# One call order in the self-attention loop: the finishing steps of a head group move behind the row-maximum steps

## The chip, the cores and the metric

The kernel runs on one core of a Trainium2 chip, in one launch. The metric is the device time of that core in microseconds (us). The kernel before takes 2647.46 us as the median of three runs (2645.61 to 2647.74).

## The reference, cut to what matters

The program computes two layers on 8 batch elements of 512 tokens with 512 features: a cross-attention layer (L0) on 77 context tokens, and then a block of self-attention, a second cross-attention and an MLP, all in float32. The change touches the self-attention alone. Its part of the reference is:

```python
NH = 16; hd = H // NH; scale = hd ** (-0.5)           # 16 heads of 32
x_norm = modulate(_ln(x), shift_a, scale_a)
q, k, v = jnp.split(x_norm @ W_qkv + b_qkv, 3, axis=-1)
attn_w = jax.nn.softmax(jnp.einsum('bhqd,bhkd->bhqk', q, k) * scale, axis=-1)   # 512 x 512 per head
attn_out = jnp.einsum('bhqk,bhkd->bhqd', attn_w, v)
attn_out = attn_out.transpose(0, 2, 1, 3).reshape(B, N, H) @ W_proj + b_proj
x = x + gate_a[:, None] * attn_out
```

## The kernel before, in words

Every engine is given its own instruction stream. One description of the order of the work (the `run` method of each stage) is walked once for each engine; each walk calls that engine's version of the same steps, and the engines meet only at semaphores. `braid` takes one step of each generator that it is given, in the order of its arguments, then the next step of each. The order of the arguments is therefore the order in which an engine finds the instructions of one step in its queue, and each engine works its queue strictly in that order.

The self-attention (class `SelfAttention`) works through 32 head groups n = 4b + g: batch element b, and four of the 16 heads in each g. A group has 16 steps (4 tiles of 128 keys or queries x 4 heads), numbered 0 to 15 here. In the braid of group n there run side by side:

- `attend(n)`: TensorE makes the scores of one key tile and head (L1871) into one of two PSUM banks, ScalarE takes their exponentials (L1949). Before steps 2, 6, 10 and 14 TensorE also makes the value sums of the key tile that is complete (L1893, with L1905 for the row sums of exponentials before steps 2 and 10), and GpSimd adds pairs of exponential tiles (L1751), one before step 10 and one at the start of the next group, right after the last exponential of this one. At the end of groups with g = 0 (from n = 4 on) GpSimd also adds the bias to the residual rows, in four instructions (L1734).
- `maxima(n + 2)`: TensorE makes the scores of the group after next the other way round (L1850) into a ring of three banks, VectorE reduces each to its negated row maxima (L1785). TensorE may write a bank again once VectorE has reduced it.
- `max_rows(n + 1)` at step 2: the maxima of the next group are turned by TensorE (L1859, which takes a bank of the same ring), copied by ScalarE (L1934), subtracted by VectorE (L1791) and sent by DMA into row 96 and 97 of the query stack.
- `finish(n - 1)`: the normalisation of the group before. ScalarE copies the value sums out of PSUM at step 2 (L1962). VectorE turns the row sums at step 10 (L1799), takes reciprocals at step 11 (L1802), spreads them at step 12 (L1805) and multiplies at step 13 (L1811). ScalarE rounds the product to the first part of a two-part number at step 14 (L1971), which stands in its queue between the exponentials of steps 14 and 15. VectorE makes the second part at step 15 (L1816).
- `project(b - 1)` in groups with g = 1, 2 and 3 from b = 1 on: the output projection of the batch element before (L389 on TensorE, gating on VectorE at L1830, adding on GpSimd at L1760). It is spread over the steps, 3 or 6 matmuls a step.

The rings that bind the engines are made in one line each:

```python
self.scores, self.max_banks, self.products = k.ring(0, 1), k.ring(2, 3, 4), k.ring(5)
self.heads, self.sums = k.ring(6), k.ring(7)
```

In ScalarE's `finish` the wait for VectorE's product stands ahead of the rounding copy:

```python
for _ in range(12):
    yield
act.wait_ge(*self.normalised(n))
...
e.copy(k.o[n % 6][:, 0, :], k.o_wide[n % 2][:]).then_inc(self.heads_hi.sem, 1)
```

Of the kernel before, what the change touches and what calls it, by code (L numbers as in the profile page):

```python
# [29 lines left out]
LAST = len(SEQ)  # L30
# [75 lines left out]
def braid(*generators):  # L106

    left = [g for g in generators if g is not None]
    while left:
        for g in list(left):  # L110
            if next(g, StopIteration) is StopIteration:
                left.remove(g)
        if left:
            yield
# [7 lines left out]
def after(steps, generator):  # L122
    for _ in range(steps):
        yield
    yield from generator


def some(steps, generator):
    for _ in range(steps):
        next(generator, None)  # L130
        yield
# [284 lines left out]
class Prepare:  # L416
# [90 lines left out]
    def run(self, s, following):  # L507
        def splits(l, first, n):
            for i in range(first, first + n):
                s.split(self.piece_at[l] + i)  # L510
                yield

        def modulations(*sources):
            for i in sources:
                yield from s.modulation(i)

        s.begin()
        s.statistics()
        yield from braid(s.context(0), after(2, splits(1, 0, G)), after(2, modulations(0)))
        yield from braid(s.keys(0), splits(1, G, G), after(1, modulations(1)))  # L520
        yield from braid(s.values(0), modulations(2, 3), some(10, following))
        yield from braid(s.context(1), some(4, following))
        yield from braid(some(9, following), splits(0, 0, 2 * G))
        yield from s.keys(1)
        yield from s.values(1)
# [1059 lines left out]
class SelfAttention:  # L1585
# [45 lines left out]
    def run(self, s, following):  # L1631

        for n in range(self.FETCH):
            s.fetch(n)
        s.load_values(0)
        yield
        yield from s.maxima(0)
        yield from braid(s.maxima(1), after(4, s.max_rows(0)))
        for n, (b, g) in enumerate(SEQ):
            if n < G:  # L1640
                s.split(self.wp_at + n)
            if n + 1 < LAST:
                s.load_values(n + 1)
            if n + self.FETCH < LAST:
                s.fetch(n + self.FETCH)
            side = []
            if g == 1 and b > 0:
                s.add_base(b - 1)
                projecting = s.project(b - 1)
            if g > 0 and b > 0:  # L1650
                tiles = (0, 1, 2, 1)[g]
                part = after(4 if g == 1 else 0, some(tiles * 4, projecting))
                side += [part] * tiles
            if n >= LAST - G - 1:
                side.append(some((1, 5, 3, 6, 8)[n - LAST], following))
            yield from braid(s.attend(n), s.finish(n - 1) if n else None, s.maxima(n + self.MAX) if n + self.MAX < LAST else None,
                             after(2, s.max_rows(n + self.ROWS)) if n + self.ROWS < LAST else None, *side)
            if g == 0 and b > 0:
                s.load_base(b - 1)
        s.values(LAST - 1, NT - 1)  # L1660
        s.sum_pair(LAST - 1, 1)
        s.load_base(B - 1)
        yield from s.finish(LAST - 1)
        yield from some(12, following)
        s.add_base(B - 1)
        yield from s.project(B - 1)
# [685 lines left out]
```

## Time and profile before

| | |
|---|---|
| median of three runs | 2647.46 us |
| the profiled execution's own time | 2647.46 us |
| its span in the trace | 2645.7 us |
| TensorE busy (matmul) | 2426.7 us, 92% |
| VectorE busy | 1388.3 us, 52% |
| ScalarE busy | 1024.6 us, 39% |
| GpSimd busy | 581.1 us, 22% |
| self-attention, first score to first score of the last group | 868.7 to 1457.1 us |

The span is the stretch that the trace covers; 1.8 us of the execution's own time lie outside it. TensorE is the engine that the chain of work that ended last runs through for 75% of the span. A busy share is an average over stages with different limits, so what an edit is worth has to be read in the self-attention stage itself. "PE" is TensorE's matmuls, "PEld" its weight loads, "DVE" VectorE, "ACT" ScalarE, "POOL" GpSimd.

### The profile page before, as it was taken

The page shows a single profiled execution, that of the slowest core. Times are in us where ns is not written, and L with a number is a line of the kernel's source. Part 1 is how long each engine was busy: PE and PEld are TensorE (multiplying, and loading weights), DVE is VectorE, ACT ScalarE, POOL GpSimd, SP SyncE. Part 2 cuts the span into 40 slices and gives each one's busy share as a digit, 9 for nine tenths or more (in the row PEclk, how much of TensorE's full clock was granted, in tenths as well). Part 3 has the DMA queues.
Part 4 walks back from the last instruction along what each step waited for, and adds up shares of the span by engine and source line. Part 5 has one row for each costly group of instructions (what it writes and reads, how often), then busy time and mean ns, then how long its engine had stood idle before and what let it go on. Part 6 is the DMA issues. An engine that isn't in the chain of part 4 may idle for free.

```text
span 2645.7 us, 32309 instructions
## 1 busy us (share of the span) xinstructions
PE 2426.7 (92%) x12048; PEld 1696.1 (64%) x12048; DVE 1388.3 (52%) x2463; ACT 1024.6 (39%) x1831; POOL 581.1 (22%) x325
## 2 busy tenths in 40 slices
PE   6678999979998899999998789999889999999998
PEld 5556666658886444444444456666578888888887
DVE  4456655464445787777777456666543222222221
ACT  2534444333332455555554233343433332332231
POOL 2001111110000356666665312111111011001100
PEclk9889999999999899999999899999999999999999
DMA  6477766645546455655553476586441101100110
GB/s 229 133 175 204 227 196 192 178 164 182 183 176 186 128 132 130 152 141 136 123 147 89 120 184 199 163 220 182 154 130 60 41 16 56 56 26 31 56 41 16
DMA packets 261227, 354.19 MB, mean 134 GB/s; under 512 B 60931, under 2 KB 109147, under 8 KB 261070
## 3 DMA queue, kind: packets, MB, share of 16 engines
q1 hardware_dynamic: 259902, 348.27, 46.2%
q0 software_dynamic: 1168, 3.85, 0.4%
q8 instruction: 96, 1.57, 0.3%
q14 instruction: 61, 0.50, 0.1%
HBM read 233.78 MB, written 116.69 MB: 132 GB/s over the span
## 4 chain that ended last, share of the span: by engine, by line
PE 75%; DVE 8%; DMA 5%; ACT 5%; issue 3%; SPq 2%; POOL 1%; DVEq 0%; ACTq 0%; POOLq 0%
PE banks L389 39%; PE banks L2150 13%; PE banks L1871 6%; PE banks L1893 4%; PE banks L1850 4%; PE banks L1905 2%; DMA norm_x<-x 1%; PE banks L1304 1%; PE banks L350 1%; PE banks L1290 1%; PE banks L1311 1%; DMA q_parts_self<-out_parts 1%; ACT wide L373 1%; DVE x_rows L1233 1%; DVE negated_max L1190 1%
## 5 line engine op out<-in xcount | busy, mean ns | idle before, releaser
L1949 ACT ACTIVATE self_exponentials<-banks 128x512 f32<-128x512 f32 x512 | 286.2, 594 | 286.3 <-PE banks L1905 137.4
L1785 DVE TENSOR_REDUCE negated_max<-banks 128x1 f32<-128x512 f32 x512 | 328.8, 676 | 104.7 <-PE banks L1850 103.2
L1751 POOL TENSOR_TENSOR self_exponentials<-self_exponentials,self_exponentials 128x2048 f32<-128x2048 f32 x64 | 294.0, 4593 | 213.7 <-ACT self_exponentials L1949 213.7
L2150 PE MATMUL banks<-mlp_w_down_hi,out_parts 128*128 128x512 f32 x1024 | 333.8, 389 | 0.1
L2106 DVE TENSOR_TENSOR out_parts<-wide,out_parts 128x512 fp32r<-128x512 f32 x128 | 93.0, 726 | 378.6 <-ACT out_parts L2179 378.6
L2169 ACT ACTIVATE wide<-banks,bias_columns 128x512 f32<-128x512 f32 x128 | 88.3, 690 | 428.0 <-PE banks L389 428.0
L1871 PE MATMUL banks<-self_query_stack,self_key_stack 98*128 98x512 f32 x512 | 234.4, 459 | 12.7 <-ACT self_exponentials L1949 6.2
L1850 PE MATMUL banks<-self_key_stack,self_query_stack 96*128 96x512 f32 x512 | 207.5, 411 | 17.8 <-DVE negated_max L1785 8.3
L1871 PEld LDWEIGHTS banks<-self_query_stack,self_key_stack 98*128 98x128 f32 x512 | 97.7, 191 | 194.8 <-ACT self_exponentials L1949 152.7
L2150 PEld LDWEIGHTS banks<-mlp_w_down_hi,out_parts 128*128 128x128 f32 x1024 | 192.2, 188 | 40.4 <-DVE x_rows L1233 0.5
L333 POOL TENSOR_SCALAR norm_rstd<-norm_mean_var 128x4 f32<-128x4 f32 x32 | 8.7, 273 | 911.1 <-DVE norm_mean_var L312 910.6
L2150 PE MATMUL banks<-mlp_w_down_lo,out_parts 128*128 128x512 f32 x512 | 199.2, 389 | 0.0
L1190 DVE TENSOR_REDUCE negated_max<-banks 128x4 f32<-128x308 f32 x256 | 120.6, 471 | 91.7 <-PE banks L389 86.8
L1893 PE MATMUL banks<-self_exponentials,self_values 128*32 128x512 f32 x1024 | 138.2, 612 | 0.5 <-ACT self_exponentials L1949 0.5
L1176 DVE SCALAR_TENSOR_TENSOR out_parts<-banks,bias_columns,out_parts 128x512 fp32r<-128x512 f32 x64 | 47.8, 747 | 145.7 <-ACT out_parts L1348 145.7
L1850 PEld LDWEIGHTS banks<-self_key_stack,self_query_stack 96*128 96x128 f32 x512 | 99.3, 194 | 36.9 <-DVE negated_max L1785 15.2
L1372 ACT ACTIVATE cross_exponentials<-banks 77x512 f32<-77x512 f32 x128 | 75.3, 591 | 122.8 <-PE banks L1290 122.6
L308 DVE BATCH_NORM_STATS2 norm_stats<-norm_x 128x6 f32<-128x512 f32 x128 | 84.6, 671 | 67.6 <-DMA norm_x<-x 61.9
L373 ACT ACTIVATE wide<-banks,modulation_columns 128x512 f32<-128x512 f32 x96 | 74.4, 775 | 108.5 <-PE banks L350 101.6
L1372 ACT ACTIVATE L_exponentials<-banks 77x512 f32<-77x512 f32 x128 | 75.3, 591 | 99.7 <-PE banks L1290 99.5
L1563 ACT ACTIVATE out_parts<-banks,bias_columns 128x512 fp32r<-128x512 f32 x64 | 44.1, 689 | 176.4 <-PE banks L389 153.7
L1149 POOL TENSOR_TENSOR x_rows<-x_rows,cross_projection_bias 128x512 f32<-128x512 f32 x32 | 44.2, 1413 | 306.0 <-DMA x_rows<-x 306.0
(201 smaller groups left out, 5405.1 us busy)
## 6 DMA issues: line engine op xcount, KB each, us to landing
L_query_stack<-q_parts_L SPq DMA_DIRECT2D x96, 256.0 KB, 4.7
x<-x_rows SPq DMA_DIRECT2D x24, 1024.0 KB, 5.0
norm_x<-x SPq DMA_DIRECT2D x24, 1024.0 KB, 7.6
self_query_stack<-q_parts_self SPq DMA_DIRECT2D x96, 256.0 KB, 4.0
self_key_stack<-k_parts_self SPq DMA_DIRECT2D x96, 256.0 KB, 6.3
x_rows<-x SPq DMA_DIRECT2D x24, 1024.0 KB, 6.1
cross_query_stack<-q_parts_cross SPq DMA_DIRECT2D x96, 256.0 KB, 4.7
q_parts_L<-out_parts SPq DMA_DIRECT2D x32, 512.0 KB, 3.9
```

Source lines behind the costliest of these rows:

```text
L373: e.activation(k.wides[w][:], bank, ACT.Identity, **kw).then_inc(self.wide.sem, 1)
L389: mm = e.matmul(out_ap, l, r, start=i == 0, stop=i == len(terms) - 1)
L1190: e.tensor_reduce(k.nm[n % 2][:, t:GH * NT:NT], k.bank[:, bk, 0:GH * S].rearrange("p (h k) -> p h k", k=S), AX_X, ALU.max, negate=True).th ...
L1372: e.activation(self.p[:, i % self.HEADS_KEPT, :], k.bank[0:S, self.scores.of["score", i], :], ACT.Exp, scale=SCALE).then_inc(self.exp.sem, 1)
L1751: e.tensor_tensor(self.p[kt - 1][:], self.p[kt - 1][:], self.p[kt][:], ALU.add).then_inc(self.paired.sem, 1)
L1785: e.tensor_reduce(k.nm[n % 2][:, h * NT + t:h * NT + t + 1], k.bank[:, self.max_banks.of["max", i], :], AX_X, ALU.max, negate=True).then_i ...
L1850: e.matmul(k.bank[:, bk, :], self.q[n % 4][0:ST, h, t * P:(t + 1) * P], self.keys[n % 4][0:ST, h, :], start=True, stop=True).then_inc(self ...
L1871: e.matmul(k.bank[:, bk, :], self.keys[n % 4][0:ST_MAX, h, kt * P:(kt + 1) * P], self.q[n % 4][0:ST_MAX, h, :], start=True, stop=True).the ...
L1893: mm = e.matmul(k.bank[h * HD:(h + 1) * HD, bk, :], self.v[n % 3][:, kt, h * HD:(h + 1) * HD], self.p[kt][:, h, :], start=kt == 0, stop=kt ...
L1949: e.activation(self.p[kt][:, h, :], k.bank[:, self.scores.of["score", i], :], ACT.Exp, scale=SCALE).then_inc(self.exp.sem, 1)
L2106: e.tensor_tensor(h[:, 1, :], k.wides[k.wide_turns.of["up", i]][:], raw(h[:, 0, :]), ALU.subtract).then_inc(self.lo.sem, 1)
L2150: mm = e.matmul(bank, l, w, start=j == 0 and q == 0, stop=j == JC - 1 and q == 2)
```

## The change

`finish(n - 1)` is passed to `braid` behind `maxima` and `max_rows` and no longer ahead of them. Nothing else is edited, and no instruction is added or dropped.

```diff
-            yield from braid(s.attend(n), s.finish(n - 1) if n else None, s.maxima(n + self.MAX) if n + self.MAX < LAST else None,
-                             after(2, s.max_rows(n + self.ROWS)) if n + self.ROWS < LAST else None, *side)
+            yield from braid(s.attend(n), s.maxima(n + self.MAX) if n + self.MAX < LAST else None,
+                             after(2, s.max_rows(n + self.ROWS)) if n + self.ROWS < LAST else None,
+                             s.finish(n - 1) if n else None, *side)
```

The queues of TensorE, GpSimd and SyncE (which issues the DMAs) hold the same instructions in the same order as before, since `finish` has nothing on them. VectorE's and ScalarE's queues change. (The edit is one line longer, so lines behind it have numbers higher by one in the changed kernel.)

On VectorE, in one group (here a group without projection), steps 3 to 15 before. `negated_max` are the reductions of `maxima`; `sums_turned`, `reciprocals_turned`, `heads_float` and `heads_parts` are the finishing instructions.

```order
L1785 TENSOR_REDUCE negated_max_83<-banks 128x1 x7
L1799 STREAM_TRANSPOSE sums_turned<-banks 128x512
L1785 TENSOR_REDUCE negated_max_83<-banks 128x1
L1802 RECIPROCAL reciprocals_turned<-sums_turned 128x16
L1785 TENSOR_REDUCE negated_max_83<-banks 128x1
L1805 STREAM_TRANSPOSE sums_turned<-reciprocals_turned 128x512
L1785 TENSOR_REDUCE negated_max_83<-banks 128x1
L1811 TENSOR_TENSOR heads_float_1_79<-heads_float_1_79,sums_turned 128x512
L1785 TENSOR_REDUCE negated_max_83<-banks 128x1 x2
L1816 TENSOR_TENSOR heads_parts_73<-heads_float_1_79,heads_parts_73 128x512
L1785 TENSOR_REDUCE negated_max_83<-banks 128x1
```

The same steps of the same group in the changed kernel:

```order
L1786 TENSOR_REDUCE negated_max_83<-banks 128x1 x8
L1800 STREAM_TRANSPOSE sums_turned<-banks 128x512
L1786 TENSOR_REDUCE negated_max_83<-banks 128x1
L1803 RECIPROCAL reciprocals_turned<-sums_turned 128x16
L1786 TENSOR_REDUCE negated_max_83<-banks 128x1
L1806 STREAM_TRANSPOSE sums_turned<-reciprocals_turned 128x512
L1786 TENSOR_REDUCE negated_max_83<-banks 128x1
L1812 TENSOR_TENSOR heads_float_1_79<-heads_float_1_79,sums_turned 128x512
L1786 TENSOR_REDUCE negated_max_83<-banks 128x1 x2
L1817 TENSOR_TENSOR heads_parts_73<-heads_float_1_79,heads_parts_73 128x512
```

Each of the five finishing instructions now stands behind the reduction of its step: the first behind the eighth reduction since step 3 and not the seventh, the last behind the reduction of step 15, at the end of the group.

On ScalarE, the start of a group before (exponentials of steps 0 to 2, the copy of the value sums, the row of maxima, the exponential of step 3):

```order
L1949 ACTIVATE self_exponentials_154<-banks 128x512 x3
L1962 COPY heads_float_0_78<-banks 128x512
L1934 ACTIVATE max_row_parts_81<-banks 16x128
L1949 ACTIVATE self_exponentials_154<-banks 128x512
L1949 ACTIVATE self_exponentials_155<-banks 128x512 x4
```

and in the changed kernel:

```order
L1950 ACTIVATE self_exponentials_154<-banks 128x512 x3
L1935 ACTIVATE max_row_parts_81<-banks 16x128
L1963 COPY heads_float_0_78<-banks 128x512
L1950 ACTIVATE self_exponentials_154<-banks 128x512
L1950 ACTIVATE self_exponentials_155<-banks 128x512 x4
```

The small copy of the maxima, which waits for TensorE's turn at L1859, has moved ahead of the copy of the value sums. The rounding copy (L1971) keeps its place between the exponentials of steps 14 and 15.

## Rows read from the trace of the kernel before

**Rows 1.** Busy by engine in the stage, granted clock, DMA share, GB/s.

```profile
868.70:1457.10 588.40, 559.25 (x2826) 265.64 (x2827) 452.94 (x715) 312.95 (x597) 356.61 (x118) 0.98 0.53 131
```

**Rows 2.** Chain of waits, end of a g = 3 group: start, us, what.

```profile
1168.90 0.61 ACT heads_parts L1971
1169.51 0.51 ACT self_exponentials L1949
...
1170.06 0.50 PE banks L1871
```

**Rows 3.** VectorE timeline, g = 2: start, us, instruction, [idle before <-releaser].

```profile
1146.09 0.72 DVE L1799 STREAM_TRANSPOSE sums_turned<-banks 128x512 f32<-128x512 f32 x1 [0.21 <-PE banks L1905]
1147.59 0.69 DVE L1785 TENSOR_REDUCE negated_max<-banks 128x1 f32<-128x512 f32 x1 [0.78 <-PE banks L1850]
...
1148.90 0.69 DVE L1805 STREAM_TRANSPOSE sums_turned<-reciprocals_turned 128x512 f32<-128x512 f32 x1
...
1150.09 0.67 DVE L1811 TENSOR_TENSOR heads_float<-heads_float,sums_turned 128x512 f32<-128x512 f32 x1
1150.69 1.28 DVE L1785 TENSOR_REDUCE negated_max<-banks 128x1 f32<-128x512 f32 x2
1151.89 0.67 DVE L1816 TENSOR_TENSOR heads_parts<-heads_float,heads_parts 128x512 fp32r<-128x512 f32 x1
```

**Rows 4.** Timeline, ScalarE, same group, steps 14 and 15.

```profile
1151.16 0.61 ACT L1971 CAST heads_parts<-heads_float 128x512 fp32r<-128x512 f32 x1
1151.67 0.60 ACT L1949 ACTIVATE self_exponentials<-banks 128x512 f32<-128x512 f32 x1
```

**Rows 5.** Timeline, GpSimd, same place.

```profile
1152.35 4.64 POOL L1751 TENSOR_TENSOR self_exponentials<-self_exponentials,self_exponentials 128x2048 f32<-128x2048 f32 x1 [3.45 <-ACT self_exponentials L1949]
```

**Rows 6.** Timeline, TensorE, the second score of the next group.

```profile
1152.65 0.40 PE L1871 MATMUL banks<-self_query_stack,self_key_stack 98*128 98x512 f32 x1
```

**Rows 7.** Timeline, VectorE, g = 3, the multiplication.

```profile
1167.82 0.67 DVE L1811 TENSOR_TENSOR heads_float<-heads_float,sums_turned 128x512 f32<-128x512 f32 x1
```

**Rows 8.** Timeline, VectorE, g = 0, the multiplication.

```profile
1110.67 1.25 DVE L1811 TENSOR_TENSOR heads_float<-heads_float,sums_turned 128x512 f32<-128x512 f32 x1
```

**Rows 9.** Timeline, GpSimd, g = 0.

```profile
1110.10 5.90 POOL L1734 TENSOR_TENSOR x_rows<-x_rows,self_gate_and_bias 128x512 f32<-128x512 f32 x4 [0.62 <-DMA self_gate_and_bias<-gate_rows]
```

**Rows 10.** Timeline, TensorE, g = 0, second score of the next group.

```profile
1113.13 0.50 PE L1871 MATMUL banks<-self_query_stack,self_key_stack 98*128 98x512 f32 x1
```

**Rows 11.** Timeline, VectorE, g = 1, multiplication, reductions 13 and 14.

```profile
1129.23 1.15 DVE L1811 TENSOR_TENSOR heads_float<-heads_float,sums_turned 128x512 f32<-128x512 f32 x1
1130.31 1.27 DVE L1785 TENSOR_REDUCE negated_max<-banks 128x1 f32<-128x512 f32 x2
```

**Rows 12.** Timeline, ScalarE, g = 1, exponential of step 15.

```profile
1130.94 0.59 ACT L1949 ACTIVATE self_exponentials<-banks 128x512 f32<-128x512 f32 x1
```

**Rows 13.** Timeline, TensorE, g = 1, start of the next group.

```profile
1130.56 0.47 PE L1871 MATMUL banks<-self_query_stack,self_key_stack 98*128 98x512 f32 x1
1131.13 0.47 PE L1850 MATMUL banks<-self_key_stack,self_query_stack 96*128 96x512 f32 x1
...
1132.82 0.40 PE L1871 MATMUL banks<-self_query_stack,self_key_stack 98*128 98x512 f32 x1
```

**Rows 14.** Waits of weight loads, 960 to 1400 us: total us, times, longest.

```profile
PEld banks L1850 <- DVE negated_max L1785: 3.7, 16, 0.3
```

**Rows 15.** Timeline, ScalarE, third group: the copy of the maxima.

```profile
918.03 0.27 ACT L1934 ACTIVATE max_row_parts<-banks 16x128 fp32r<-16x128 f32 x1 [2.03 <-PE banks L1859]
```

**Rows 16.** Timeline, VectorE, the multiplication in the last groups.

```profile
1474.45 4.43 DVE L1811 TENSOR_TENSOR heads_float<-heads_float,sums_turned 128x512 f32<-128x512 f32 x1
```

**Rows 17.** Timeline, GpSimd, same place.

```profile
1473.77 4.56 POOL L1751 TENSOR_TENSOR self_exponentials<-self_exponentials,self_exponentials 128x2048 f32<-128x2048 f32 x1
```

**Rows 18.** Timeline, VectorE, g = 0 at 964 us.

```profile
964.50 0.67 DVE L1811 TENSOR_TENSOR heads_float<-heads_float,sums_turned 128x512 f32<-128x512 f32 x1
```

**Rows 19.** Timeline, GpSimd, same place.

```profile
964.48 4.76 POOL L1734 TENSOR_TENSOR x_rows<-x_rows,self_gate_and_bias 128x512 f32<-128x512 f32 x3 [1.17 <-DMA self_gate_and_bias<-gate_rows]
```

## The prediction

> **What bounds the kernel now.** I first read the busy time of the stage that is edited. TensorE is busy for 559.25 of 588.40 us at a granted clock of 0.98, that is 2.4 GHz for nearly all of it [rows 1]. VectorE has 452.94 us and ScalarE 312.95 us, so neither is the bound by its sum; either costs time only where TensorE has run up to it. I then read the chain of waits. At the end of a group with g = 3 it leaves TensorE and goes through ScalarE: the rounding copy of 0.61 us (L1971), the exponential of step 15, and then, 0.04 us after its end, the next group's second score on TensorE [rows 2]. That copy waits for VectorE's multiplication (L1811). So the date of the multiplication is what the edit is to be judged by, and for it I read the timelines of the four engines in one group of each kind (g = 0 to 3), which repeat from n = 4 on with the same durations.
>
> In a g = 2 group before, VectorE has a gap while TensorE makes sums. It runs the first finishing instruction (L1799, 0.72 us) in it, at 1146.09, and still waits 0.78 us before reduction 10 at 1147.59. The multiplication starts at 1150.09, 2.50 us after reduction 10 [rows 3]. It ends at 1150.76, and ScalarE, busy with the exponential of step 14, takes the product up at 1151.16 without a wait [rows 4].
>
> **The change, part by part.** No instruction is added, so all cost is in waits. It acts in the braids that have both `finish` and `maxima`, n = 1 to 29, and on ScalarE's step 2 in n = 1 to 30.
>
> *VectorE, steps 10 to 13.* The first finishing instruction now stands behind reduction 10, which starts when its scores are there, at 1147.59 as before. Two things come in between reduction 10 and the multiplication: that instruction, which leaves the hidden gap, and reduction 13. In a full queue each starts some 0.07 us before the one ahead ends: the pair of reductions 13 and 14 takes 1.20 us from its start to the next instruction, 0.60 each [rows 3], and 0.72 becomes 0.65. So the multiplication starts 2.50 + 0.65 + 0.60 = 3.75 us after reduction 10, at 1151.34, and ends at 1152.01, 1.25 us later than before. The following is what hangs on it, by kind of group.
>
> - g = 2, six groups (n = 6 to 26). ScalarE's copy moves from 1151.16 to 1152.01, 0.85 us. The exponential of step 15 started 0.51 us behind it and takes 0.60 [rows 4], so it now ends at 1153.12. TensorE wanted to start the second score at 1152.65, behind projection matmuls [rows 6]; it starts at about 1153.17, and the weight load that had been hidden shows for another 0.1 us. 0.6 us each, 3.6 us.
> - g = 3 (six groups, n = 7 to 27) and n = 1 to 3, which have no projection either: nine. The multiplication ended at 1167.82 + 0.67 = 1168.49 [rows 7] and will end at 1169.74; the copy moves from 1168.90 by 0.84 us. TensorE has no cover here: its score followed the exponential by 0.04 us [rows 2]. 0.85 us each, 7.7 us.
> - g = 0, seven groups (n = 4 to 28). GpSimd's four adds run here [rows 9], and the multiplication takes 1.25 us in place of 0.67 [rows 8], since it waits for one of them. It ended at 1111.92 and the score came at 1113.13 [rows 10], right behind the exponential. 1.25 us later it meets the next of the adds in the same phase, so I take the whole 1.25 and give back 0.15 for reductions that are ready sooner afterwards. 1.1 us each, 7.7 us.
> - g = 1, seven groups (n = 5 to 29). The multiplication took 1.15 us since GpSimd's pair was still running; it started at 1129.23 and ended at 1130.38 [rows 11]. At 1130.48 that pair is over: 0.67 us, end 1131.15, 0.77 us later. The exponential moves from 1130.94 to 1131.71 and ends at 1132.30 [rows 12], ahead of the score at 1132.82, which six projection matmuls cover [rows 13]. Nothing is lost. TensorE gains: its L1850 at 1131.13 came 0.57 us behind the score at 1130.56, right after reduction 13 (1130.31 to 1130.98) [rows 11, 13]. Reduction 13 is now ahead of the multiplication and ends at about 1130.55. I take 0.25 us each, a gain of 1.8 us.
>
> *VectorE, step 15.* The last finishing instruction (L1816) goes behind reduction 15. Nobody waits for it soon (ScalarE reads its flag two groups later, the projection at the start of the next g = 1). Its new date is a rival below.
>
> *ScalarE, step 2.* The copy of the value sums now stands behind the small copy of maxima. Where TensorE's turn is in time, the two only swap and the exponential of step 3 starts as before. In the first groups it is late: the small copy waited 2.03 us [rows 15], and the value sums were copied during that wait. They now come after it, so step 3's exponential is later by about the length of such a copy, 0.5 us (0.61 for the one in rows 4, less overlap), in three groups: 1.5 us. The row of maxima is late for nobody otherwise, since it has fourteen steps until `attend(n + 1)` reads it. TensorE's, GpSimd's and SyncE's queues are as they were, so no transfer moves except with them.
>
> Sum: 3.6 + 7.7 + 7.7 - 1.8 + 1.5 = 18.7 us. Everything behind a late TensorE follows TensorE, so nothing gives it back. The profiled execution took 2647.46 us, the same as the median, so the forecast is 2666 us. The bounds: if the first finishing instruction finds a gap elsewhere, each delay shrinks by its 0.65 us and the sum falls to about 5 us, which is no change by the measure below; if no slack covers anything (1.25 us in all 29 groups) it is 36 us. I take the middle value because the rows for it are exact repeats from one batch element to the next.
>
> **Rivals.**
>
> *The last finishing instruction runs into GpSimd (slower still).* By the sum, L1816 starts three slots behind the multiplication, at 1151.34 + 1.80 = 1153.14. GpSimd starts the pair 0.08 us after the exponential of step 15 has ended (1152.35 against 1152.27) [rows 4, 5], so now at 1153.20. Before, L1816 was 0.46 us ahead of it [rows 3, 5]; now 0.06 us. Such a VectorE instruction that starts behind the pair waits for all of it: 4.43 us with the pair at 1473.77 [rows 16, 17] in place of 0.67. For VectorE's winning speaks the one tie that the trace has: at 964.50, 0.02 us after a GpSimd add of the same kind began, it took its plain 0.67 us [rows 18, 19]. If it loses, L1816 ends some 4.6 us late with the next group's reductions behind it. TensorE goes on meanwhile on sums and on its three banks; I let 2 to 3 us of each reach it, 2.6, in the fifteen groups of g = 2, g = 3 and n = 1 to 3: 39 us, or 2705 us. It decides at a shift of the order of 0.1 us, and it can hold for some groups only.
>
> The Trainium skill, page "SBUF — State Buffer", section "SBUF: two separate sides", states the rule behind it: the port pair shared by VectorE and GpSimd is an exclusive lock, and whichever instruction starts first holds it until it is done. By that rule a VectorE instruction in front costs only GpSimd half a microsecond, and one behind the pair costs VectorE all of it. The trace agrees (4.43 us against 0.67).
>
> *No change.* The late product is absorbed before it reaches TensorE, as in g = 1. For it speaks VectorE's spare time (452.94 of 588.40 us). Against it, the g = 3 chain has 0.04 us between exponential and score. Time 2647 to 2650 us.
>
> *Faster.* The reductions go first, so banks come free sooner, and ScalarE isn't late because the multiplication finds a gap. But TensorE's weight loads wait for reductions for 3.7 us in sixteen places between 960 and 1400 us, 0.3 us at most [rows 14]; with the 1.8 us of g = 1, of which these are in part the same, about 5.5 us can be had: 2642 us.
>
> **How the numbers follow.** Forecast 0.72; collision 0.14; no change 0.09; faster 0.05. A difference of under 0.2% (5.3 us) can't be told from none here. The forecast's own range is 2656 to 2676 us. The range to 2690 us takes in a collision in some of the groups, and its lower end is 2655 us. Slower 0.86, same 0.09, faster 0.05.
>
> **What would show it.** In the changed trace: the multiplication starts about 3.75 us after reduction 10; ScalarE now has a wait for VectorE's multiplication in front of the rounding copy, 0.7 to 0.8 us in g = 1, 2 and 3 and about 1.3 us in g = 0 (there was next to none). Four groups together take some 2.3 us more, out of 0.85 + 0.6 + 1.1 - 0.25. The pairs of GpSimd that start behind L1816 take about 5.1 us and not 4.64; if instead L1816 takes 5 us, the collision has come. If the copy shows no wait, the forecast is wrong at its root.

## The result and the profile of the changed kernel

The changed kernel takes 2665.53 us as the median of four runs (2660.66 to 2667.67), the kernel before 2646.53 us beside it (four runs, 2643.4 to 2647.74). The ratio is 1.0072 with a 95% interval of 1.0053 to 1.0089: slower by some 19 us; the forecast was 2666 us. The profiled execution took 2660.24 us, with a span of 2658.4 us.

The stage first, as in [rows 1]: busy time of each engine, granted clock, DMA share, GB/s, from the first score to the first score of the last group.

```profile
867.78:1476.60 608.82, 565.44 (x2827) 266.69 (x2827) 445.38 (x715) 314.71 (x597) 361.87 (x118) 0.97 0.51 126
```

It takes 608.82 us in place of 588.40, 20.4 us more, for the same work (2826 and 2827 matmuls recorded). TensorE's busy time grew by only 6.2 us: the rest is waiting.

VectorE's timeline in a g = 2 group (n = 14), which answers to [rows 3]; columns are start, us, instruction, and in brackets the idle time before it and what ended it.

```profile
1159.36 0.69 DVE L1786 TENSOR_REDUCE negated_max<-banks 128x1 f32<-128x512 f32 x1 [1.70 <-PE banks L1851]
1159.97 0.71 DVE L1800 STREAM_TRANSPOSE sums_turned<-banks 128x512 f32<-128x512 f32 x1
...
1162.49 0.65 DVE L1786 TENSOR_REDUCE negated_max<-banks 128x1 f32<-128x512 f32 x1
1163.07 0.67 DVE L1812 TENSOR_TENSOR heads_float<-heads_float,sums_turned 128x512 f32<-128x512 f32 x1
1163.66 1.28 DVE L1786 TENSOR_REDUCE negated_max<-banks 128x1 f32<-128x512 f32 x2
1164.86 0.68 DVE L1817 TENSOR_TENSOR heads_parts<-heads_float,heads_parts 128x512 fp32r<-128x512 f32 x1
```

VectorE now idles 1.70 us in one piece ahead of reduction 10, where it had done the first finishing instruction and idled 0.21 and 0.78 us. Everything behind is one full queue, and the multiplication starts 1163.07 - 1159.36 = 3.71 us after reduction 10 (2.50 before).

The same place on the three other engines, in the order ScalarE, GpSimd, TensorE ([rows 4 to 6] before).

```profile
1163.77 0.62 ACT L1972 CAST heads_parts<-heads_float 128x512 fp32r<-128x512 f32 x1 [0.70 <-DVE heads_float L1812]
1164.30 0.59 ACT L1950 ACTIVATE self_exponentials<-banks 128x512 f32<-128x512 f32 x1
...
1164.96 5.01 POOL L1752 TENSOR_TENSOR self_exponentials<-self_exponentials,self_exponentials 128x2048 f32<-128x2048 f32 x1 [4.29 <-ACT self_exponentials L1950]
...
1164.94 0.50 PE L1872 MATMUL banks<-self_query_stack,self_key_stack 98*128 98x512 f32 x1 [0.30 <-ACT self_exponentials L1950]
```

ScalarE waits 0.70 us for the product, the exponential of step 15 ends at 1164.89, and TensorE, which had projection matmuls to do, idles 0.30 us before the score that needs it. The end of the next group (g = 3), ScalarE and then TensorE, answers to [rows 2]:

```profile
1182.11 0.62 ACT L1972 CAST heads_parts<-heads_float 128x512 fp32r<-128x512 f32 x1 [0.70 <-DVE heads_float L1812]
1182.64 0.59 ACT L1950 ACTIVATE self_exponentials<-banks 128x512 f32<-128x512 f32 x1
...
1183.28 0.50 PE L1872 MATMUL banks<-self_query_stack,self_key_stack 98*128 98x512 f32 x1 [1.02 <-ACT self_exponentials L1950]
```

Here there is no projection, and TensorE idles 1.02 us: its score again follows the exponential at once (1183.23 to 1183.28).

The waits between 960 and 1400 us (total us, times, longest), of the changed kernel:

```profile
PEld banks L1872 <- ACT self_exponentials L1950: 131.5, 225, 2.5
PE banks L1872 <- ACT self_exponentials L1950: 17.0, 23, 2.2
```

and of the kernel before:

```profile
PEld banks L1871 <- ACT self_exponentials L1949: 116.3, 222, 0.8
PE banks L1871 <- ACT self_exponentials L1949: 3.0, 13, 0.3
```

TensorE's own waits for exponentials grew from 3.0 to 17.0 us, the longest from 0.3 to 2.2 us. The other side of the trade can be read as well: weight loads that waited for reductions, 3.7 us before [rows 14], have no entry in this stretch any more.

### The profile page after: what moved, and what is told of

Its sections match the earlier page's. It is cut to its first block and busy times, and to the rows that moved or that the text cites. A ratio compares the mean times of both kernels' runs of the same rounds, so it can differ in the third digit from the quotient of the medians.

```text
span 2658.4 us, 32309 instructions
## 1 busy us (share of the span) xinstructions
PE 2434.8 (92%) x12048; PEld 1696.6 (64%) x12048; DVE 1381.1 (52%) x2463; ACT 1027.0 (39%) x1831; POOL 586.4 (22%) x325
## 5 line engine op out<-in xcount | busy, mean ns | idle before, releaser
L1752 POOL TENSOR_TENSOR self_exponentials<-self_exponentials,self_exponentials 128x2048 f32<-128x2048 f32 x64 | 302.5, 4726 | 228.0 <-ACT self_exponentials L1950 228.0
L389 PE MATMUL banks<-cross_w_p_hi,heads_parts 128*128 128x512 f32 x256 | 96.6, 418 | 15.9 <-DVE x_rows L1233 15.8
```

The costliest lines, as they stand in the source:

```text
L389: mm = e.matmul(out_ap, l, r, start=i == 0, stop=i == len(terms) - 1)
L1752: e.tensor_tensor(self.p[kt - 1][:], self.p[kt - 1][:], self.p[kt][:], ALU.add).then_inc(self.paired.sem, 1)
```

## The experiments

In the first four, the kernel before took 2645.89 us (median of 23 runs on the same chip), in the fifth to seventh 2648.18 us (17 runs), in the last two 2644.67 us (one run). Line numbers are those of each kernel. The code is cut to what moves, with `...` for lines left out; its comments are added here. Groups are counted from n = 0, so the third group is n = 2. "Behind" a group means the period that starts with the next group's first score, since that is where a late end shows.

**Which engine's queue carries the cost.** `braid` can be given `finish` ahead on one engine and behind on the other; a field says which.

```diff
+            ahead = s.finish(n - 1) if n and s.ahead else None
+            behind = s.finish(n - 1) if n and not s.ahead else None
+            yield from braid(s.attend(n), ahead, s.maxima(...), after(2, s.max_rows(...)), behind, *side)
```

The new order on ScalarE alone (`ahead=True` on VectorE):

> Only ScalarE's queue has the new order (small copy of the maxima ahead of the copy of the value sums at step 2); VectorE's is that of before. My theory (the loss is VectorE's late multiplication): 1 to 2 us slower than before, all of it in the first three groups, ratio 1.0000 to 1.0010. Rival (ScalarE's order is what costs, 0.5 us in each of 30 groups): 15 us slower, ratio 1.0057.

Measured: 2647.54 us (12 runs), ratio 1.0001 (0.9987 to 1.0016). In its trace the third and fourth group (n = 2 and 3) take 1.65 and 0.85 us more and no later group more than 0.05 us, up to n = 28. The new order on VectorE alone:

> Only VectorE's queue has the new order. My theory: nearly the whole loss, 16 to 19 us slower than before (ratio 1.006 to 1.007), with ScalarE waiting 0.7 to 0.8 us for the multiplication in each group. Rival (ScalarE's order costs): 3 us or less.

Measured: 2667.08 us (5 runs), ratio 1.0084 (1.0065 to 1.0104), with the multiplication 3.71 us after reduction 10 and ScalarE's wait at 0.70 to 0.73 us with g = 1, 2 and 3 (1.09 to 1.42 us with g = 0). The cost is VectorE's; ScalarE's swap is paid in two groups only.

**Only the first finishing instruction late.** The transpose of the row sums alone goes behind reduction 10; the other four stay ahead.

```diff
-            dve.wait_ge(*self.summed(2 * n + 1))
-            e.transpose(k.turned[:], k.bank[:, self.sums.of["sums", n], :]).then_inc(self.sums_turned.sem, 1)
+        def finish_late(n):          # given to braid behind max_rows
+            for _ in range(10):
+                yield
+            dve.wait_ge(*self.summed(2 * n + 1))
+            e.transpose(k.turned[:], k.bank[:, self.sums.of["sums", n], :]).then_inc(self.sums_turned.sem, 1)
```

> Order of before, but the first finishing instruction (the transpose of the sums, step 10) stands behind reduction 10; the others stay ahead of theirs. My theory: the multiplication is 0.65 us late in place of 1.25, of which ScalarE's own lateness hides 0.4. About 0.3 us in the nine groups without projection, 0 in g = 2, 0.1 in g = 1, and in g = 0 between 0.1 and 1.25 us, as the multiplication meets one of GpSimd's adds or the next: 3 to 12 us slower, 7 as the middle (ratio 1.0027). Rival (each late microsecond of the multiplication costs the same, no threshold): 0.52 of the whole, 10 us.

Measured: 2668.66 us (6 runs), ratio 1.0081 (1.0062 to 1.0100), as much as the whole change: a miss of the expected range, and above its rival too. Outside g = 0 the product path went as expected (multiplication 3.26 us after reduction 10, ScalarE's wait 0.25 to 0.28 us, 0.40 us more behind g = 3). The largest part of the loss is behind g = 0, 10.7 of the 20.4 us by which the stage grew: in six of these seven groups the multiplication took 1.49 to 1.74 us beside GpSimd's adds and ScalarE waited 1.08 to 1.33 us, and behind three of them, two of which lost 2.6 and 2.7 us, the granted clock fell as well (0.58 to 0.66 over 4 us). And behind g = 2, where nothing was expected, it is 0.58 us each, 3.5 us. VectorE and TensorE at the end of a g = 2 group:

```profile
1013.10 0.67 DVE L1811 TENSOR_TENSOR heads_float<-heads_float,sums_turned 128x512 f32<-128x512 f32 x1
1013.69 1.28 DVE L1787 TENSOR_REDUCE negated_max<-banks 128x1 f32<-128x512 f32 x2
...
1013.70 0.48 PE L1877 MATMUL banks<-self_query_stack,self_key_stack 98*128 98x512 f32 x1
1014.52 0.47 PE L1856 MATMUL banks<-self_key_stack,self_query_stack 96*128 96x512 f32 x1 [0.34 <-DVE negated_max L1787]
```

There is a second path from VectorE to TensorE, through the ring of three banks. Reduction 13 stands behind the multiplication here, starts at 1013.69, and the next scores for maxima (L1856) wait for it: they come 0.82 us behind the score at 1013.70, where the distance is 0.30 us when nothing waits (1163.22 and 1163.52 in the changed kernel). In the changed kernel reduction 13 has gone ahead of the multiplication, so the change lengthens the product path and shortens this one, where this edit lengthens both. The prediction spoke of the second path as a gain in g = 1; that it also bounds the loss in other groups is seen in this run. Over the stretch from 960 to 1400 us TensorE's matmuls of this kind waited 13.1 us for reductions here, 0.4 us in the kernel before.

**Only the multiplication late**, behind reduction 13, by the same means:

```diff
+        def finish_late(n):
+            for _ in range(13):
+                yield
+            w = k.o_wide[n % 2]
...
+            e.tensor_tensor(w[:], w[:], k.turned[:], ALU.mult).then_inc(self.normalised.sem, 1)
```

> Order of before, but the multiplication alone (step 13) stands behind reduction 13. My theory: it is 0.60 us late, ScalarE hides 0.4 of it, 0.25 us in nine groups are lost (2 us); in g = 0 and g = 1 the multiplication comes out of its wait for GpSimd at the same time as before and reduction 13 is early, which gives back up to 0.25 us in seven groups of g = 1: between 2 us faster and 5 us slower, middle +1 (ratio 1.000). Rival (no threshold): 0.48 of the whole, 9 us slower.

Measured: 2651.54 us (12 runs), ratio 1.0015 (1.0002 to 1.0027). The steady groups went as worked out (3.11 us, ScalarE's wait 0.09 to 0.13 us, 0.23 us more behind g = 3, 0.02 behind g = 2, 0.30 less behind g = 1). Not expected was g = 0: the multiplication, 0.60 us later, fell among GpSimd's four adds and took 1.62 to 1.79 us in five of the seven groups with g = 0. Behind four of the five the granted clock fell (0.57 to 0.62 over 4 us), and three of these periods are 2.35 to 2.83 us longer. The stage is 10.4 us longer in this trace and the whole execution only 1.7 us, so the ratio says less about the stage here than the trace does. VectorE, GpSimd and TensorE in one of the three:

```profile
1113.61 1.78 DVE L1822 TENSOR_TENSOR heads_float<-heads_float,sums_turned 128x512 f32<-128x512 f32 x1
...
1112.32 5.87 POOL L1736 TENSOR_TENSOR x_rows<-x_rows,self_gate_and_bias 128x512 f32<-128x512 f32 x4 [0.51 <-DMA self_gate_and_bias<-gate_rows]
...
1116.59 0.50 PE L1877 MATMUL banks<-self_query_stack,self_key_stack 98*128 98x512 f32 x1 [1.54 <-ACT self_exponentials L1955]
```

**Only the last finishing instruction late**, behind reduction 15. Without the delay of the others it starts 0.12 us behind GpSimd's pair, where in the changed kernel it is 0.1 us ahead: this makes the collision of the first rival.

```diff
+        def finish_late(n):
+            for _ in range(15):
+                yield
...
             dve.wait_ge(*self.heads_hi(n))
+            e.tensor_tensor(o[:, 1, :], k.o_wide[n % 2][:], raw(o[:, 0, :]), ALU.subtract).then_inc(self.heads_lo.sem, 1)
```

> Order of before, but the last finishing instruction alone (L1816, step 15) stands behind reduction 15. My theory (the collision of the prediction): nothing delays the exponential of step 15 here, so GpSimd's pair starts as before, 0.46 us behind the old place of the instruction, and its new place is 0.60 us further back, so 0.1 us behind the pair. In the nine groups without projection and the six of g = 2 it takes about 5 us in place of 0.67, and 2 to 3 us of each reach TensorE: 39 us slower (20 to 70), ratio 1.008 to 1.026. Rival (the place of the last instruction is free, since nobody waits for it soon): no change, or up to 3 us faster from reduction 15.

Measured: 2712.56 us (4 runs), ratio 1.0231 (1.0207 to 1.0256), 61 us by the ratio; within the expected range, above its middle. VectorE, GpSimd and TensorE at the end of a g = 3 group:

```profile
1035.58 4.97 DVE L1822 TENSOR_TENSOR heads_parts<-heads_float,heads_parts 128x512 fp32r<-128x512 f32 x1
1040.48 1.87 DVE L1787 TENSOR_REDUCE negated_max<-banks 128x1 f32<-128x512 f32 x3
...
1035.45 4.55 POOL L1753 TENSOR_TENSOR self_exponentials<-self_exponentials,self_exponentials 128x2048 f32<-128x2048 f32 x1 [3.45 <-ACT self_exponentials L1955]
...
1041.21 0.38 PE L1865 MATMUL banks<-identity,negated_max 128*16 128x128 f32 x1 [2.53 <-DVE negated_max L1787]
```

The instruction ends 0.55 us after the pair, the reductions of the next group stand behind it, TensorE idles 2.53 us, and the group from that point runs at a lower mean clock:

```profile
1034.52:1055.48 20.96, 18.14 (x81) 7.57 (x82) 17.14 (x21) 10.12 (x19) 11.65 (x5) 0.84 0.61 163
```

It takes 20.96 us where the same group took 16.20 before. The Trainium skill's page "SBUF — State Buffer", section "SBUF: two separate sides", says that whichever of the two engines starts first keeps the shared port pair for its whole instruction; this case's rows agree on both sides of the tie, with VectorE's instruction at 0.68 us when 0.10 us ahead and at 4.97 us when 0.13 us behind. Closer than that the recorded starts don't decide: in [rows 18, 19] VectorE's instruction started 0.02 us behind an add and took its plain 0.67 us.

**ScalarE's copy out of the way.** If the cost is the exponential of step 15 standing behind a copy that waits, it must go when the copy moves behind that exponential. The last finishing instruction, which needs the copy, then has to move as well, into the next group, so this run changes two places and not one.

```diff
-            for _ in range(12):
+            for _ in range(13):          # ScalarE's finish: the copy behind exponential 15
...
+        def second(n):                   # VectorE, given n - 2 and ahead of maxima
+            for _ in range(0 if n % G == G - 1 else 6):
+                yield
```

> The changed order on both engines, but ScalarE's rounding copy stands behind the exponential of step 15 and not ahead of it, and the last finishing instruction of VectorE, which needs the copy, comes in the next group (step 6, in groups with g = 1 step 0), when GpSimd's pair is over. My theory (the loss comes through ScalarE's wait ahead of the last exponential): the 19 us are gone and some more, as the copy itself is no longer in the way where there is no projection: 5 us faster than before (8 faster to 2 slower), ratio 0.998. Rival (the loss is VectorE's order as such, its reductions being late for TensorE): still 10 us or more slower than before.

Measured: 2642.35 us (12 runs), ratio 0.9984 (0.9968 to 1.0000). VectorE's multiplication is as late as in the changed kernel (3.71 us), and yet the period behind g = 3 is what it was before (+0.06 us at most up to n = 23), behind g = 2 too (+0.01), and behind g = 1 it is 0.30 to 0.35 us less (up to n = 25). Only behind g = 0, where GpSimd's adds meet the late instructions, it still costs 0.1 to 0.8 us (1.2 in the last). The end of a g = 3 group (n = 15), ScalarE's copy and then TensorE:

```profile
1166.61 0.62 ACT L1980 CAST heads_parts<-heads_float 128x512 fp32r<-128x512 f32 x1 [0.23 <-DVE heads_float L1815]
...
1166.59 0.39 PE L1880 MATMUL banks<-self_query_stack,self_key_stack 98*128 98x512 f32 x1
1167.23 0.50 PE L1859 MATMUL banks<-self_key_stack,self_query_stack 96*128 96x512 f32 x1 [0.26 <-DVE negated_max L1789]
```

The copy still waits for the product, 0.23 us, but the score at 1166.59 no longer waits for ScalarE, where it waited 1.02 us in the changed kernel. That wait, and with it the loss against the kernel before, came by way of ScalarE's queue. It doesn't follow that VectorE's lateness is free: the second path is now what TensorE waits for, 0.26 us at 1167.23, and between 960 and 1400 us weight loads waited 13.7 us for reductions (3.7 before).

**Both paths freed.** The transpose, reciprocal and spread stand ahead of the reductions as in the kernel before, the multiplication goes behind reduction 14, the copy and the last instruction as in the experiment above.

```diff
+            yield from braid(s.attend(n), s.second(n - 2) if n > 1 else None, s.finish(n - 1) if n else None,
+                             s.maxima(...), after(2, s.max_rows(...)), s.multiply(n - 1) if n else None, *side)
...
+        def multiply(n):
+            for _ in range(14):
+                yield
```

> As e6, but the first three finishing instructions stand ahead of their reductions as before, in the gap that TensorE's sums leave, and the multiplication stands behind reduction 14. ScalarE's small copy at step 2 is as before the change. My theory: 0.46 us less in each of nine groups, 0.7 in seven of g = 0, 0.3 in seven of g = 1, nothing in g = 2: 11 us faster than before (4 to 14), ratio 0.996. If GpSimd's adds delay the multiplication in g = 0 past reduction 15's date, 5 us of it go. Rival (TensorE has no such slack and the date of the last exponential is hidden elsewhere): no change.

Measured: 2637.31 us (5 runs, 2635.82 to 2640.08), ratio 0.9957 (0.9943 to 0.9970), faster than the kernel before, and so than the changed one, by more than the interval. The stage:

```profile
872.01:1453.98 581.97, 555.44 (x2827) 267.52 (x2827) 446.72 (x715) 315.15 (x597) 359.81 (x118) 0.97 0.53 132
```

The stage is 6.4 us shorter (588.40 before), where 11 us had been worked out. The period behind g = 3 is 0.47 to 0.49 us less than before (up to n = 23), which the moved copy gives with reductions on time, 0.24 to 0.83 us less behind g = 0 (up to n = 24) and 0.30 to 0.33 less behind g = 1 (up to n = 25). But the third and fourth group, where 0.46 us less each was expected, took 2.00 and 0.51 us more, at a granted clock of 0.83. That execution took 2637.1 us, 10.4 less than the profiled one before; the other 4 us lie outside the stage (3.3 more ahead of it, 7.3 less behind its last group's first score), and what lies outside differs by more than that between profiles, as the next experiment shows. So the median's 11 us fit the expectation partly by luck.

**The changed kernel twice more**, to see what of its trace belongs to the order and what to the execution.

> The changed kernel itself, its call written on one line fewer. In its first profile the self-attention stage takes 20.4 us more from the first score to the first score of the last group, of which 5.0 us lie in the first three groups and 3.5 in the group after n = 4, each beside a stretch at the lower granted clock, and 6.4 us come back in the cross stage. Theory A: the steady terms (multiplication 3.71 us after reduction 10, ScalarE's wait 0.7 us, periods +0.83 behind g = 3, +0.60 behind g = 2, -0.3 behind g = 1) belong to the order and repeat within 0.03 us; the stretches at the lower clock and what comes back later belong to the execution and move. Theory B: the low stretches belong to the order too (the waits are just long enough to cause them) and come at the same groups again. Time 2660 to 2668 us.

> The same kernel once more, for the same question: what of the 20.4 us of the stage and of the 6.4 us that come back behind it repeats. By A the stage's difference lies between 17 and 22 us with the low stretches elsewhere; by B it is 20 to 21 us with them at the same groups. Time 2660 to 2668 us.

Measured: 2669.44 and 2664.16 us (one run each). The stage and the third group (n = 2) in the second profile:

```profile
873.47:1482.92 609.45, 565.17 (x2826) 266.71 (x2827) 443.46 (x715) 314.60 (x597) 362.14 (x118) 0.96 0.51 126
915.75:937.15 21.40, 18.87 (x82) 6.76 (x82) 17.61 (x24) 10.54 (x20) 9.54 (x2) 0.84 0.42 100
```

and in the third:

```profile
868.15:1477.52 609.37, 565.59 (x2827) 267.03 (x2827) 443.32 (x715) 314.74 (x597) 361.96 (x118) 0.96 0.51 126
910.44:931.83 21.39, 18.91 (x82) 6.72 (x82) 17.60 (x24) 10.54 (x20) 9.54 (x2) 0.84 0.43 100
```

The second took 1.4 us more than the expected range, the third lies in it. The steady terms repeat within 0.03 us. Theory B holds for the low stretches: in all three profiles the third, fourth and sixth group are longer by 2.74 to 2.76, 2.30 to 2.33 and 2.68 to 3.53 us, each with a stretch at the lower clock (in the fourth the kernel before has a shorter one as well). The stage repeats within 0.7 us (+20.4, +21.1, +21.0). What lies outside it does not: span less stage is 2057.3 us before, and 2049.6, 2058.2 and 2053.0 us in the three profiles of the changed kernel. So the first profile's 7.7 us less outside the stage is that execution's and no effect of the order; the stage's 20 to 21 us is what the medians' 19 us are made of.

## Why the prediction was right, and where it was not

The forecast of 2666 us stands against 2665.5 measured, and its root (a wait for VectorE's multiplication ahead of ScalarE's rounding copy, paid by TensorE) is shown by the trace, by VectorE's order alone costing all of it, and by TensorE's wait going away with the copy's move. That the number fits to half a microsecond is luck: the stage grew by 20.4 to 21.1 us where 18.7 had been worked out, and the terms missed in both directions. By its steps, from the first profile; "longer" is a group's period from first score to first score against before:

| step | predicted | measured |
|---|---|---|
| reduction 10 to multiplication | 3.75 us | 3.71 us in every group |
| wait ahead of the copy, g = 1, 2, 3 | 0.7 to 0.8 us | 0.69 to 0.73 us |
| the same, g = 0 | about 1.3 us | 0.77 to 1.83 us |
| behind g = 3 and n = 3 (7 groups) | 0.85 us each | 0.83 us each (0.74 once), 5.7 us |
| behind g = 2 (6) | 0.6 us each | 0.61 us each, 3.6 us |
| behind g = 1 | -0.25 us each, -1.8 us | -0.30 to -0.33 us each, +0.17 once, -1.75 us |
| behind g = 0 (7) | 1.1 us each, 7.7 us | 0.3 to 1.03 us in six, 3.53 in one, 7.7 us |
| behind n = 1 and 2, with ScalarE's swap | 0.85 each and 1.5 | 2.74 and 2.30 us |
| four groups together (behind g = 0, 1, 2 and 3) | 2.3 us | 1.7 to 2.1 us in five of six, 4.7 in the first |
| sum in the stage | 18.7 us | 20.4 us |

**The steady terms**, behind g = 1, 2 and 3, came out because each was a distance between two rows moved by a known amount and cut where TensorE had cover; the projection matmuls cover 0.25 us of 0.85 in g = 2.

**g = 0: the sum is right by luck and the working is not.** The step that failed is that the later multiplication meets the next of the adds in the same phase. The 1.25 us of [rows 8] was one group's number and no repeating one: in the seven groups of the kernel before the multiplication took 0.67 (the one of [rows 18]), 1.14, 1.25, 1.18, 1.25, 1.06 and 1.33 us. In the changed kernel it takes 0.73 to 1.24 us in five of the seven, as the adds' start moves against it (it follows a DMA, by the bracket of [rows 9]). Those groups lost 0.60 to 1.03 us, and the last, with 1.53 us, lost 0.31 net. What they lacked against 1.1 us came back in one place, behind n = 4. VectorE, GpSimd and TensorE there:

```profile
970.68 1.80 DVE L1812 TENSOR_TENSOR heads_float<-heads_float,sums_turned 128x512 f32<-128x512 f32 x1
...
969.42 5.42 POOL L1735 TENSOR_TENSOR x_rows<-x_rows,self_gate_and_bias 128x512 f32<-128x512 f32 x4 [1.13 <-DMA self_gate_and_bias<-gate_rows]
...
973.69 0.70 PE L1872 MATMUL banks<-self_query_stack,self_key_stack 98*128 98x512 f32 x1 [2.16 <-ACT self_exponentials L1950]
974.19 0.63 PE L1851 MATMUL banks<-self_key_stack,self_query_stack 96*128 96x512 f32 x1
974.75 1.94 PE L1906 MATMUL banks<-self_exponentials,ones 128*32 128x512 f32 x8
```

TensorE idled 2.16 us, and then the granted clock is 0.57 over 4 us:

```profile
973.70:977.70 4.00, 4.00 (x18) 0.99 (x18) 2.89 (x3) 0.90 (x2) 4.00 (x2) 0.57 1.05 209
```

Eight row-sum matmuls take 1.94 us in place of 1.06. Waits worked out as delays, at the full clock throughout, can't give this: such a wait is paid a second time. The length of the wait alone doesn't decide it. TensorE of the same trace behind n = 20 idled 1.59 us and went on at full clock, with the same eight matmuls at 1.07 us:

```profile
1275.83 0.51 PE L1872 MATMUL banks<-self_query_stack,self_key_stack 98*128 98x512 f32 x1 [1.59 <-ACT self_exponentials L1950]
...
1276.51 1.07 PE L1906 MATMUL banks<-self_exponentials,ones 128*32 128x512 f32 x8
```

In the two later profiles the wait behind n = 4 was 1.44 and 1.27 us, and the clock fell there too; the seven periods behind g = 0 sum to 7.3 and 7.2 us in them, again with a third or more of it behind n = 4.

**The first groups: a term mis-sized, since the lower clock was left out.** Predicted was 3.2 us (0.85 twice and ScalarE's swap at 0.5 in three groups); measured 5.0. TensorE of the changed kernel at the start of n = 2:

```profile
911.83 0.50 PE L1872 MATMUL banks<-self_query_stack,self_key_stack 98*128 98x512 f32 x1 [1.03 <-ACT self_exponentials L1950]
912.17 0.45 PE L1851 MATMUL banks<-self_key_stack,self_query_stack 96*128 96x512 f32 x1
912.55 1.94 PE L1906 MATMUL banks<-self_exponentials,ones 128*32 128x512 f32 x8
```

and of the kernel before:

```profile
911.86 0.50 PE L1871 MATMUL banks<-self_query_stack,self_key_stack 98*128 98x512 f32 x1 [0.21 <-ACT self_exponentials L1949]
912.20 0.40 PE L1850 MATMUL banks<-self_key_stack,self_query_stack 96*128 96x512 f32 x1
912.53 1.06 PE L1905 MATMUL banks<-self_exponentials,ones 128*32 128x512 f32 x8
```

The longer wait is the 0.85 us of the sum. The group's mean granted clock is 0.84 in the later profiles above, and the eight matmuls alone take 0.88 us more. Why 1.03 us of idling is followed by the lower clock here, and the same 1.02 us behind g = 3 and the 1.59 us behind n = 20 are not, stays open; no run was made for it.

**ScalarE's swap** was expected in three groups at 0.5 us. In the run with that part alone it shows in two, 1.65 and 0.85 us, with a stretch at the lower clock in the first and a longer one than before in the second, and is not seen in the whole time (1.0001).

**The last finishing instruction** kept ahead of GpSimd by 0.10 to 0.11 us (predicted 0.06) and the pairs take 4.96 to 5.02 us (predicted 5.1). The rival was real: with 0.13 us on the other side it costs about 61 us. The prediction's 39 us for it was low. In that run's stage the fifteen groups that it meant lost 44 us (2.9 each and not 2.6), and the seven periods behind g = 0, which it left out, another 14: the multiplication took 1.83 to 1.85 us beside the adds in five of these groups and 4.28 us in one, and the clock fell behind all six.

**No change and faster** fell with the g = 3 chain: 0.04 us of slack before, 0.05 us after. The gain that the "faster" rival spoke of is there (-0.33 us behind g = 1), and it shows in the whole time only once the copy stands elsewhere: in the run with both paths freed the kernel is 11 us faster by the medians, 6.4 us of it seen in the stage.

## What to carry to other kernels

When an instruction moves back in one engine's queue, follow its product into the next engine's queue and ask what stands behind the instruction that waits for it: VectorE had 135 us to spare here, and 1.2 us of it cost 19 us because an exponential stood behind a copy. Most of the cure here was to let the waiting copy pass behind the work that TensorE needs; the rest came from keeping VectorE's reductions on time. And follow all paths of the late engine, not only the one that is edited: the buffers that it frees are a second one.

## What the runs showed of the hardware that was not expected

- TensorE's clock fell to its lower level (1.2 GHz) behind waits of 1.03 and 2.16 us in the changed kernel and of 1.54 us in the run with the multiplication late, inside a stage in which it is busy for 93 to 95% of the time; the stretch after the 2.16 us has a granted clock of 0.57 in place of 1.00, and eight matmuls took 1.94 us in place of 1.06. It did not fall behind the 1.02 us waits after g = 3, nor behind waits of 1.59 us (behind n = 20) and, in the second profile of that kernel, 1.81 us (behind n = 24). With VectorE's order alone it fell behind a 1.04 us wait after one g = 3 group (n = 27) and not after the six before it. In three profiles of the same kernel it fell in the same three groups, the third, fourth and sixth, though the wait at the start of the sixth was 2.16, 1.44 and 1.27 us.
- Who gets past whom between VectorE and GpSimd's pair is decided within 0.25 us: 0.10 us ahead VectorE's instruction takes 0.68 us and GpSimd's 5.0 (4.64 before), 0.13 us behind VectorE's takes 4.97 us and ends 0.55 us after GpSimd's, and GpSimd's takes 4.55.
- Among four GpSimd adds back to back, VectorE's multiplication is mostly not held for all of them: 1.80 us at the most in the changed kernel, ended 0.55 us after the running add, so it gets in between two. But that is no rule: in one group (n = 20) of the run with the last finishing instruction late it took 4.28 us, to 0.55 us after the last add, and ScalarE waited 3.14 us for it.

```profile
1299.94 4.28 DVE L1813 TENSOR_TENSOR heads_float<-heads_float,sums_turned 128x512 f32<-128x512 f32 x1
...
1298.69 4.98 POOL L1736 TENSOR_TENSOR x_rows<-x_rows,self_gate_and_bias 128x512 f32<-128x512 f32 x4
```
